# Retention's first tokens, projections, scores and decays issued before the last hidden transposes of the FP4 stage ahead of it

## What is computed

```
x = x + 0.5 * fp4_ffn(layernorm(x))        # stage 3
x = x + retention(layernorm(x))            # stage 4
x = x + 0.5 * fp4_ffn(layernorm(x))        # stage 5
fp4_ffn(x): g = q(x) q(w_gate)^T; u = q(x) q(w_up)^T; return q(silu(g) * u) q(w_down)^T
            # q rounds blocks of 16 to FP4 with the block's largest magnitude as scale
retention:  Q, K, V = x Wq, x Wk, x Wv     # 16 heads of 8
            scores[l, m] = (Q K^T)[l, m] * gamma_h^(l - m) / sqrt(8), 0 for m > l
            out = scores V; normalised per head over its 8 channels and all 1024 tokens; then Wout
```

## Time and profile before

| | us |
|---|---|
| median of 3 runs (lowest, highest) | 1823.05 (1821.37, 1827.81) |
| the profiled execution's own time | 1822.8 |
| its span from first to last instruction | 1820.9 |
| PE busy | 1648.1 (91%) |
| DVE busy | 1403.6 (77%) |
| ACT busy | 990.0 (54%) |
| POOL busy | 345.4 (19%) |
| mean granted TensorE clock | 0.948 of full |

### The profile page before, as it was taken

How to read it: one execution, slowest core, us unless ns; L and a number is a source line. 1 busy time by engine, 2 the same in 40 slices (tenths; PEclk the granted TensorE clock), 3 DMA queues, 4 the chain that set the end, 5 groups by cost and what they waited for, 6 DMA issues and landing times.

```text
span 1820.9 us, 30152 instructions
## 1 busy us (share of the span) xinstructions
PE 1648.1 (91%) x10801; PEld 962.1 (53%) x10801; DVE 1403.6 (77%) x2337; ACT 990.0 (54%) x1958; POOL 345.4 (19%) x661
## 2 busy tenths in 40 slices
PE   6899999879999999999999888999997787998686
PEld 5788888621111111111111257888886565665565
DVE  5755555789999999999999266555576985999895
ACT  3232234338888888888888742233323543654452
POOL 5310002460000001000000320100010234344211
PEclk9899999979999999999999999999998887999788
DMA  3000000121110100011010001000000000000000
GB/s 129 1 1 0 0 0 18 57 83 38 32 30 24 37 22 22 24 40 32 28 37 10 8 6 53 1 0 0 0 1 1 0 1 0 2 2 2 1 24 24
DMA packets 25301, 35.91 MB, mean 20 GB/s; under 512 B 5808, under 2 KB 19696, under 8 KB 24672
## 3 DMA queue, kind: packets, MB, share of 16 engines
q1 hardware_dynamic: 25184, 34.38, 6.3%
HBM read 22.57 MB, written 8.78 MB: 17 GB/s over the span
## 4 chain that ended last, share of the span: by engine, by line
PE 74%; DVE 12%; ACT 5%; issue 4%; POOL 3%; DMA 0%; POOLq 0%; SPq 0%; ACTq 0%; DVEq 0%
PE PS L963 13%; PE PS L432 12%; PE PS L951 10%; PE PS L421 6%; PE PS L422 6%; PE PS L423 6%; PE PS L940 5%; ACT probs L1035 3%; DVE neg_half L1098 3%; PE PS L1541 3%; PE PS L1621 2%; PE PS L1556 2%; POOL qk_all L1468 2%; PE PS L1631 1%; DVE qk_all L1319 1%
## 5 line engine op out<-in xcount | busy, mean ns | idle before, releaser
L1098 DVE TENSOR_REDUCE neg_half<-PS 128x2 f32<-128x1024 f32 x512 | 601.6, 1220 | 39.7 <-PE PS L940 24.6
L1035 ACT ACTIVATE probs<-PS 128x512 f32<-128x512 f32 x1024 | 528.9, 603 | 112.3 <-PE PS L951 112.2
L515 ACT ACTIVATE shared<-PS 128x512 f32<-128x512 f32 x256 | 152.6, 597 | 374.3 <-PE PS L423 361.5
L951 PE MATMUL PS<-qk_all 51*128 51x512 bf16 x1024 | 279.6, 387 | 17.9 <-ACT probs L1035 12.6
L609 DVE TENSOR_TENSOR shared<-shared,PS 128x512 f32<-128x512 f32 x256 | 174.0, 686 | 156.4 <-ACT shared L515 154.7
L963 PE MATMUL PS<-probs,Vg 128*32 128x512 f32 x2048 | 274.5, 608 | 0.1
L432 PEld LDWEIGHTS PS<-wd,shared 128*128 128x128 f32 x2048 | 249.5, 193 | 11.3 <-issue 0.5
L432 PE MATMUL PS<-wd,shared 128*128 128x128 f32 x2048 | 250.7, 276 | 0.0
L951 PEld LDWEIGHTS PS<-qk_all 51*128 51x128 bf16 x1024 | 71.6, 93 | 338.5 <-ACT probs L1035 319.4
L940 PE MATMUL PS<-qk_all 48*128 48x512 bf16 x1024 | 193.7, 390 | 17.1 <-DVE neg_half L1098 14.9
L617 DVE SCALAR_TENSOR_TENSOR x<-PS,gates,x 128x128 f32 (+1 forms) x512 | 144.0, 344 | 71.6 <-PE PS L432 71.6
(11 more groups left out here) (210 smaller groups left out, 2101.7 us busy)
## 6 DMA issues: line engine op xcount, KB each, us to landing
split<-qk_all SPq DMA_DIRECT2D x16, 384.0 KB, 3.2
qk_all<-split SPq DMA_DIRECT2D x64, 96.0 KB
qk_all<-split SPq DMA_DIRECT2D x64, 64.0 KB
qk_all<-split SPq DMA_DIRECT2D x64, 32.0 KB
shared<-OTs SPq DMA_DIRECT2D x60, 32.0 KB
probs<-in_ret_const SPq DMA_DIRECT2D x1, 1538.5 KB, 7.1
qk_all<-negT SPq DMA_DIRECT2D x96, 4.0 KB, 1.7
SC<-inverse SPq DMA_DIRECT2D x3, 512.0 KB, 5.0
```

Of the source, the lines that this page charges most:

```text
L515: act.activation(sg[:, f, :], bank(f), ACT.Silu).then_inc(s["silu"], 1)
L951: pe.matmul(bank(RING_AT + use % RING), qs[rows, slot, 1, pair, kt * P:(kt + 1) * P], qs[rows, slot, 0, pair, half * GW:(half + 1) * GW], ...
L1035: act.activation(probs[:, n % 2, STRIPS * strip + pair, :], bank(RING_AT + use % RING), ACT.Exp, scale=ATT_SCALE).then_inc(s["exped"], 1)
L1098: dve.tensor_reduce(neg_half[m % 2][:, i % 2, :, at], bank(use_bank(i, m), 2).rearrange("p (s w) -> p s w", s=STRIPS), AX.X, ALU.max, nega ...
```

## The change

The four retention programs become generators with one `yield`, and each stage-3 program takes one as `lead` and advances it once. On ACT the lead runs behind the last `ffn_hidden_anchor` and before `hiddenT(7)`: `centre` and `scale` of tiles 0 to 3, `turned` 0 and 1, `projected(0)`. On PE it runs behind `down(6)` and before `hiddenT(7)`: `transposeT` and `project` of 0 and 1, and `score(0)`. On DVE it runs between the statistics of group 6 and `add(7)`: `masks(0)` and the four `decay(0)`. On POOL `vm(0)` stands between `ln_finish` of group 6 and of group 7. New waits: PE waits for all products of stage 3 before the lead and for `add(7)` before `update(0)`; DVE waits for the last `hq` before its lead. The buffers of the lead are moved to where the end of stage 3 no longer reads or writes: `qm` and `rxn` over `hraw`, `pj` and `rxT` behind `hqT`; `ft2` shrinks from 1408 to 768 columns. No DMA is added or moved, and no computation is added or left out.

```diff
-        hraw, ft1, ft2, hq = (carve(HW) for _ in range(4))
+        hraw, ft1, ft2, hq = carve(HW), carve(HW), carve(max(GU_TILES * P, HW // 2)), carve(HW)
...
-        rxn, rxT = (carve(2 * P).rearrange("p (u w) -> p u w", u=2) for _ in range(2))
+        qm = carve(2 * JH * P).rearrange("p (u j w) -> p u j w", u=2, j=JH)
+        rxn = carve(2 * P).rearrange("p (u w) -> p u w", u=2)
+        assert taken[0] <= HW
         qd, kd = (carve(3 * P).rearrange("p (u w) -> p u w", u=3) for _ in range(2))
-        pj = carve(12 * P).rearrange("p (u w) -> p u w", u=3)
-        kT, vs = pj[:, :, P:2 * P], pj[:, :, 3 * P:4 * P]
-        qm, vm = (carve(2 * JH * P).rearrange("p (u j w) -> p u j w", u=2, j=JH) for _ in range(2))
+        vm = carve(2 * JH * P).rearrange("p (u j w) -> p u j w", u=2, j=JH)
...
+        taken[0] = hqT_end
+        pj = carve(12 * P).rearrange("p (u w) -> p u w", u=3)
+        kT, vs = pj[:, :, P:2 * P], pj[:, :, 3 * P:4 * P]
+        rxT = carve(2 * P).rearrange("p (u w) -> p u w", u=2)
...
@@ ffn_dve
                 ln_stats(dve, GROUPS - 2)
+                dve.wait_ge(s["hq"], GROUPS)
+            next(lead, None)
             add(GROUPS - 1)
@@ ffn_pool
                 for g in range(GROUPS - 3, GROUPS):
+                    if g == GROUPS - 1:
+                        next(lead, None)
                     ln_finish(pool, 4, g)
@@ ffn_pe
+            pe.wait_ge(s["h"], (c0 + GROUPS) * PAIRS)
+            next(lead, None)
             for c in range(len(CHUNKS)):
                 hiddenT(GROUPS - 1, c)
             down(GROUPS - 1)
@@ ret_pe
-                if c == 0:
-                    wait(pe, s["state"], b * STATES)
+                if k == 0:
+                    pe.wait_ge(ffn["added"], GROUPS)
+                elif c == 0:
+                    pe.wait_ge(s["state"], b * STATES)
...
+            pe.wait_ge(ld["ret"], 32)
+            pe.wait_ge(ld["wret"], 32)
             transposeT(0)
             transposeT(1)
             project(0)
             project(1)
+            score(0)
+            yield
             transposeT(2)
             project(2)
             transposeT(3)
-            score(0)
@@ ret_act
             centre(3)
+            scale(3)
+            yield
             projected(1)
-            scale(3)
             turned(2)
@@ ret_dve
             masks(0)
+            for g in range(HG):
+                decay(0, g)
+            yield
             masks(1)
             for k in range(CHUNKS_ALL):
                 b, c = k // BT, k % BT
-                wait(dve, s["o_ps"], k - 1)
-                for g in range(HG):
-                    decay(k, g)
+                if k > 0:
+                    wait(dve, s["o_ps"], k - 1)
+                    for g in range(HG):
+                        decay(k, g)
@@ the tensor program; the other three are changed alike
-            ffn_pe(pe, 3)
-            pe.wait_ge(ld["ret"], 32)
-            pe.wait_ge(ld["wret"], 32)
-            ret_pe(pe)
+            retention = ret_pe(pe)
+            ffn_pe(pe, 3, retention)
+            for _ in retention:
+                pass
             ffn_pe(pe, 5)
```

More of the change, by code:

```diff
@@ L166, in macaron @@
         taken[0] = ROOM // 2 - 2 * GW - GW // 2 - 2 * (NB_T + GT * NB_I)
-        tokens_at = taken[0]
+        hqT_end, tokens_at = len(CHUNKS) * GW + 3 * HW + max(GU_TILES * P, HW // 2), taken[0]
         xq, tcode = carve(GW), carve(GW)
@@ L186, in macaron @@
         moments, gm, gvar, grstd = carve(2), carve(4), carve(1), carve(1)
+        assert taken[0] <= hqT_end
+        taken[0] = hqT_end
+        pj = carve(12 * P).rearrange("p (u w) -> p u w", u=3)
+        kT, vs = pj[:, :, P:2 * P], pj[:, :, 3 * P:4 * P]
+        rxT = carve(2 * P).rearrange("p (u w) -> p u w", u=2)
         assert taken[0] <= tokens_at
@@ L1418, in ffn_pieces, with ffn_dve @@
                 to, src = to + w, src + w
-        def ffn_dve(dve, link, n):
+        def ffn_dve(dve, link, n, lead=iter(())):
             s = ffn
@@ L1458, in ffn_dve, with ffn_pool @@
                 ln_stats(dve, GROUPS - 1)
-        def ffn_pool(pool, n):
+        def ffn_pool(pool, n, lead=iter(())):
             s = ffn
@@ L1470, in ffn_pool, with ffn_act @@
                 for g in range(GROUPS - 3, GROUPS):
+                    if g == GROUPS - 1:
+                        next(lead, None)
                     ln_finish(pool, 4, g)
-        def ffn_act(act, n):
+        def ffn_act(act, n, lead=iter(())):
             s = ffn
@@ L1518, in ffn_act, with ffn_pe @@
                     tokensT(g + 2)
+            next(lead, None)
             for c in range(len(CHUNKS)):
                 hiddenT(GROUPS - 1, c)
-        def ffn_pe(pe, n):
+        def ffn_pe(pe, n, lead=iter(())):
             s = ffn
@@ L1919, in _ @@
             moe_pool(pool, 2)
-            ffn_pool(pool, 3)
             pool.wait_ge(ld["ret"], 32)
-            ret_pool(pool)
+            retention = ret_pool(pool)
+            ffn_pool(pool, 3, retention)
+            for _ in retention:
+                pass
             ffn_pool(pool, 5)
@@ L1930, in _ @@
             fp4_weights_act(act)
-            ffn_act(act, 3)
-            ret_act(act)
+            retention = ret_act(act)
+            ffn_act(act, 3, retention)
+            for _ in retention:
+                pass
             ffn_act(act, 5)
@@ L1953, in _ @@
                 pass
-            ffn_dve(dve, link, 3)
-            ret_dve(dve, chain, link)
+            retention = ret_dve(dve, chain, link)
+            ffn_dve(dve, link, 3, retention)
+            for _ in retention:
+                pass
             ffn_dve(dve, link, 5)
```

## The result

| | before | after |
|---|---|---|
| median, us (runs) | 1823.11 (5) | 1808.20 (5) |
| lowest, highest | 1821.37, 1827.81 | 1806.92, 1820.12 |
| profiled execution's own time, span | 1822.8, 1820.9 | 1820.12, 1818.2 |
| mean granted clock | 0.948 | 0.946 |

The ratio of after to before is 0.9924, with a 95% interval of 0.9896 to 0.9953: faster by 0.5 to 1.0% (the two medians alone give 0.9918). The forecast was 1810.3 in 1806 to 1816.5.

The account below looks back on a forecast made before the run. Serial work at the border from stage 3 to retention was taken as the bound: 18.58 us becomes 6.7 (gain 11.9), `down(7)` ends 0.9 earlier, together 12.8 off 1822.8, plus 0.25 for the median: 1810.3, range 1806 to 1816.5.

Parts of the forecast that it names:

- What bounds the border: From stage 3 to retention: 18.58 us of serial work between the end of `down(7)` and `outputs(1)`, while engines idled earlier.
- D: Landmark at the border: the end of `down(7)`, stage 3's last matmul group; at 1527.23 us before the change.
- Step 1: The lead on ACT and PE behind `down(6)`: transposes start at 1513.9 and `score(0)` can start at 1517.4.
- Step 2: `score(0)` in front delays `hiddenT(7)` by 0.4 to 1.5 us; the lead's parts on ACT, DVE and POOL stay hidden.
- Step 3: End of `down(7)`: between 1525.1 and 1528.7 depending on PE's clock; 1526.3 taken, 0.9 us earlier than before.
- Step 4: From D to `outputs(1)`: 18.58 us becomes 6.7, gaining 11.9, with PE's and POOL's chains late together.
- Step 5: Moved buffers and the shorter `ft2`: costed at nothing, within a few tenths of a microsecond either way.
- the gain comes through whole: Behind the border: PE stays busy for 132.43 of 139 us, so the full 12.8 us gained should reach the end.
- the lead would do nothing: Rival: a wait starts the lead late, 13.6 us of prologue stay on the path, 1818 to 1824; chance 0.08.
- slow-clock rival: Rival: a PE pause at the border lets the clock fall, gain 6.4 to 8 us, 1815 to 1817; chance 0.22.
- slower rival: Rival: retention's loop enters at clock 0.50 and stays, about 3 us more per chunk, 1825 to 1831; chance 0.04.

Follow-up runs that it names:

- E1: Kernel before the change with only the changed kernel's buffer placement, order of work as before; ratio to before 0.9991.
- E3: Kernel before the change with 24 unused identity transposes added on PE between `down(6)` and `hiddenT(7)`; ratio to before 0.9994.
- E2: Changed kernel with `score(0)` back behind `down(7)` and `decay(0)` behind `add(7)`; ratio to before 0.9930.
- E7: Changed kernel with `transposeT(2)` and `turned(2)` also in the lead and `project(2)` between `hiddenT(7)` and `down(7)`; median 1804.24 us, ratio to before 0.9886.
- E10: Changed kernel with `vm(0)` and `vm(1)` both ahead of `ln_finish` of group 6; ratio to before 0.9881.
- E6: Changed kernel with `vm(1)` as well ahead of `ln_finish` of group 7; ratio to before 0.9893 from two runs.
- E4: Changed kernel with POOL's `vm(0)` back behind `ln_finish` of group 7; ratio to before 0.9950.
- E5: Changed kernel with DVE's `masks(0)` and `decay(0)` back behind `add(7)` and its statistics; ratio to before 0.9940.
- E9: Changed kernel with four more 128x512 copies on ACT in the lead ahead of `projected(0)`, lengthening PE's pause; ratio to before 0.9911.
- E0: Changed kernel run again with nothing altered; median 1811.58 us of 10 runs, ratio to before 0.9925.
- E8: Changed kernel with `transposeT(2)`, `turned(2)`, `project(2)` moved ahead of `down(7)`'s end and both `vm` ahead of `ln_finish(6)`; median 1805.28 us, ratio to before 0.9879.

## Why the prediction was right

- *What bounds the border.* Right. The prologue was on the path as serial work, and E1 and E3 leave it there at 18.57 and 18.58 us behind D, whatever the buffers or the clock ahead of it.
- *Step 1.* Right: `score(0)` began 8.26 us behind the start of `down(6)`; the prediction had 1517.4 - 1509.15 = 8.25.
- *Step 2.* Right: `hiddenT(7)` at 9.33 behind `down(6)`, where 9.45 was the early end; E2 puts the cost of `score(0)` in front at 0.3. DVE's and POOL's parts were hidden as told: DVE still waited 3.14 before `add(7)`, and POOL's `ln_finish(7)` ended 5.1 behind D, where 5.3 was told.
- *Step 3.* The mechanism was right, the size was off. The term was "`hiddenT(7)` to the start of `down(7)` is 3.64", taken from a row at the lower clock for both ends; with the clock up it was 1532.18 - 1529.45 = 2.73. So D lay 15.00 us behind the start of `down(6)`, earlier than the best end, 15.95, and 2.15 us earlier than the middle that I took. Of these 2.15, 0.95 is the mis-sized term and 1.2 is the choice of the middle between the two levels of the clock. The clock did not vary there: `down(7)` took 2.9 in all ten profiles with the lead in any form.
- *Step 4.* Right: `outputs(0)` at D + 2.74 (2.8 told), `outputs(1)` at D + 6.50 (6.7 told). PE and POOL ended side by side there, 0.1 apart. That shortening one of them alone gives nothing is E7 for PE (6.65 behind D) and E10 for POOL (6.42); E6 (7.11) brought a collision of its own. E4 and E5 show that neither POOL's nor DVE's part could have been left.
- *Step 5.* Right by E1.
- *That the gain comes through whole* failed. "What is gained at the border should come through whole" looked only at who waits for whom. The prediction named a port among the things that it might have overlooked, but priced it at nothing; a shift between engines changes which instructions meet at a shared port. 1.08 us went at `outputs(2)`, which E10 shows to be the masks' work. Another 0.8 went at a later chunk, where in the profile after, DVE's mask of 1.31 us stands beside a `vm`; that this is the cause there is read from these rows and was not tested by itself:

```profile
1580.05 1.27 POOL L1773 TENSOR_TENSOR qk_all<-qk_all,probs 128x512 f32<-128x512 f32 x1
1580.16 1.31 DVE L1797 TENSOR_TENSOR qk_all<-qk_all,probs 128x128 f32<-128x128 f32 x1 [0.49 <-ACT qk_all L1723]
```

The two errors have opposite signs: 2.1 too little for D and 0.2 behind it against 1.9 lost later and 0.4 found in stage 5. So 12.8 us were told and 13.7 are found from `down(6)` to the end, and that they lie so near is in part luck: with the right D and nothing lost later, the same sum gives 15.2. The medians differ by 14.9, within what the spread of the runs allows. That the lead would do nothing is ruled out by steps 1 and 2. The slow-clock rival did not come; in E9, with 3.35 us of waiting before `score(0)`, the clock fell, and the price was lower than that rival had it. The slower rival found nothing in its favour.

## What to carry to other kernels

Between two stages, the serial start of the next one can stand in the tail of the last, where each engine idles in turn; leaving out DVE's part gave back a sixth of the gain at the border here and POOL's a third (ACT's and PE's were not left out as a whole). Price such a move by the waits, and then once more by which VectorE instructions with two SBUF inputs will newly run beside POOL's: look in the trace before for instructions of one kind that take longer beside the other engine. And where runs scatter by more than the effect, compare intervals between landmarks in the profiles: in the two profiles of the changed kernel the border repeats to 0.01 us, while its ten times in E0 spread over 16.

## What the runs showed of the hardware that was not expected

- From the start of `down(6)` to the end of the span, thirteen profiles of twelve different kernels gave only 311.8, 308.4, 301.5, 298.1 and 294.7 us, each within 0.1, steps of 3.4 or twice that, though the border interval moved by fractions of a microsecond between them. They do not follow the border interval (21.06, 21.42, 21.76 and 22.10 end at 294.7, but the change with 21.50 at 298.1). They do follow the start of `outputs(2)`, counted from that of `down(6)`: 24.8 to 25.8 ends at 294.7, 26.3 at 298.1, 27.1 to 30.2 at 301.5, 37.0 at 308.4 and 40.4 at 311.8. What lies between is given back behind it. Part of the giving back is in stage 5: from retention's last add to the end it took 131.63 in E2 and 130.20 in E4, which had reached that add 1.4 us later. Stage 5's chain of waits goes through POOL's `hq`, `hiddenT`, half of `gate_up`, ACT and two roundings on DVE in each group, as in these rows of the changed kernel, and the granted clock changes inside each group (0.66 and 1.00 below):

```profile
1736.81 2.60 POOL qk_all L1475
...
1739.45 2.95 PE PS L1566 x12
1742.40 2.78 PE PS L1551 x12
...
1745.86 1.38 ACT qk_all L1320
...
1747.26 1.64 DVE qk_all L1323
...
1750.62 2.60 POOL qk_all L1475
```
```profile
1740.00:1744.00 4.00, 4.00 (x19) 3.18 (x18) 3.86 (x6) 2.41 (x4) 0.00 (x0) 0.66 0.00 0
1744.00:1748.00 4.00, 4.00 (x23) 3.21 (x23) 3.60 (x5) 2.28 (x4) 0.00 (x0) 1.00 0.00 0
```

  That the changes of the clock hold each group to them, and so make the steps, fits these rows but was not tested: it is argued, not shown.
- Why E10 ends 3.4 us before the change can be added up from its steps: 1.2 us by `outputs(2)`, which are the masks, 1.6 at the tenth step of `outputs`, 0.8 at the eleventh, and 0.2 given back later. The tenth step lies just behind the start of the second sequence, and its 1.6 us are the clock: E6, E7, E8 and E10 take 3.93 us for it instead of 5.52 to 5.54 before and after, and `outputs(9)` itself takes 1.08 in E10, 1.60 after and 1.93 before. The stretch in it, after first, then E10:

```profile
1576.00:1577.00 1.00, 1.00 (x16) 0.62 (x7) 0.95 (x2) 0.00 (x0) 0.00 (x0) 0.50 0.00 0
```
```profile
1568.00:1569.00 1.00, 1.00 (x33) 0.81 (x32) 1.00 (x3) 0.00 (x0) 0.00 (x0) 1.00 0.09 16
```

  PE has the same pause, 1.0 us ahead of `score(10)` for DVE's decays, in both. Why the clock fell behind it in one and not in the other stays open.
- The spread of the times comes from ahead of the border: `down(6)` started between 1503.86 and 1520.12 in the profiles, with the same instructions before it. Two profiles of the one changed kernel differ there by 9.0 us (1520.12 and 1511.11).
